# Constants multiplied on TensorE in the waits of a four-block convolution kernel

## The chip, the cores and the metric

The kernel runs on one core of a Trainium2 chip. Its engines are TensorE (PE: matmuls, whose weight loads, PEld, are shown apart), VectorE (DVE), ScalarE (ACT), GpSimd (POOL) and SyncE (SP, which here issues DMAs). The metric is the time of one execution on the device in microseconds (us), the median over runs.

## The reference

x is (4, 32, 256, 256) in float32. Four blocks follow one another, each on a group-normalised image (16 groups of 2 channels), each added to its input:

```python
x = x + _L0_conv_ref(_gn(x), w, bias)      # x and w rounded to 8-bit integers, 3x3 convolution, scaled back
x = x + _L1_conv_ref(_gn(x), w1, w2)       # real part of the 2-d FFT, 64x32 low modes mixed over channels, back
x = x + _L2_conv_ref(_gn(x), conv_w, b)    # 1x1 product; its 5x5 pooled means are then the filter of a 5x5 convolution
x = x + _L3_conv_ref(_gn(x), conv_w, ...)  # maxima of 3x3 patches (over channels, rows, columns), 201 -> 1152 product,
                                           # norm, relu; times the patch, mean over its 9 pixels; 2x2 outputs a pixel
```

## The kernel before

One image at a time (b = 0 to 3) is held in on-chip memory as 128 partitions: 32 channels by the four parities of row and column, each of 128 x 128 pixels. A tile is 4 rows, 128 x 512 elements, one bank of PSUM; there are 32 tiles (NT). Every engine has its own program, written out by hand, and they meet at semaphores: an engine waits with `wait_ge`, another counts up with `then_inc`. PSUM has 8 banks; bank 6 is also the small one (`sbk`).

Ahead of the images one pass over x finds maxima and sums, from which scales and the matrix `taps0` (9 blocks of 128 x 128 in bfloat16, the quantised 3x3 weights laid out by parity) are made. `taps0` is not written again.

TensorE's program for an image, in order, with its lines:

- L440, quantised convolution, 9 matmuls a tile into banks 0 to 3, as soon as DVE has quantised the rows (L1075, L1077). ACT scales the result (L649), DVE adds it to the image (L1086).
- L450, transposes of the image, four to a bank (banks 2 to 5), copied by ACT (L655) and DVE (L1101). L477 and L463 are the two transforms, L427 the group's statistics (`group_stats`), L484 and L485 small ones.
- Mixing of channels is done by DVE and POOL (L1135, L893, L1139). TensorE then spreads the result in two bursts (L495, h = 0 and 1), for which DVE's L1139 is waited for; DVE's L1144 follows.
- L507 and L517, the inverse transforms; DVE adds the wave to the image (L1163) and pools it (L1168), ACT takes sums (L681, L683).
- L427 (statistics again), then L523 and L524 (25 columns and 1) and L527, which make the filter; DVE and ACT form and split the taps (L1233, L732, L1240, L1241).
- L544, the second convolution, 36 matmuls for each of 16 blocks of 8 rows. ACT copies a part (L706), DVE combines (L1262, L1265, L1269). After it L427 for the last norm, and ACT normalises the image (L756, eight parts).
- L555, transposes of which DVE takes maxima (L1323), meanwhile DVE and ACT begin the first patch tiles (L1313 to L1319, L763, L764, L771); L559; ACT and DVE finish the maxima, which go through memory and back by DMA.
- L575, the product stage: 45 matmuls for each of 32 tiles, DVE multiplies (L1348), POOL and DVE add (L929, L1353, L1357), SP stores.

The loops L440, L544 and most of L575 run as loops on the chip, the rest is written out for each image.

Of the kernel before, what the change touches and what calls it, by code (L numbers as in the profile page):

```python
# [17 lines left out]
P = 128  # L18
# [17 lines left out]
NBLK = HO // RP  # L36
# [49 lines left out]
def build(nc, x, w0, b0, w2, w2t, b2, mixw, w3a, w3b, bn, cst, out):  # L86
    with ExitStack() as ctx:  # L87
        def sb(name, n, dt=F32):
            return ctx.enter_context(nc.sbuf_tensor(name, [P, n], dt))

        def sem(name):
            return ctx.enter_context(nc.semaphore(name))
# [9 lines left out]
        taps0 = sb("taps0", 9 * P, BF16)  # L102
# [19 lines left out]
        def cs(name, p0=0, p1=P):  # L122
            return consts[p0:p1, CST[name][0]:CST[name][1]]
# [85 lines left out]
        def urow(t, i):  # L209
            return t[:, UN * i:UN * i + UN].rearrange("p (r w) -> p r w", w=PW)  # L210
# [41 lines left out]
        s_u, s_uh, s_ul, s_third, s_mid, s_sum2, s_sum1, s_clear, s_ones = (  # L252
            sem("s_u"), sem("s_uh"), sem("s_ul"), sem("s_third"), sem("s_mid"), sem("s_sum2"), sem("s_sum1"), sem("s_clear"), sem("s_ones"))
# [16 lines left out]
        V, A, G, T = nc.vector, nc.scalar, nc.gpsimd, nc.tensor  # L270
# [138 lines left out]
        def _(pe):  # L409
            def bank(n):  # L410
                return psum[:, n, :]

            def image_row(r):
                return img[:, r * PW + 1:r * PW + 1 + WO]
# [10 lines left out]
            def group_stats(b, g):  # L425
                pe.wait_ge(s_gnin, b * 3 + (g + 1))
                T.matmul(sbk[:, 0:2], cs("group"), mv, start=True, stop=True).then_inc(s_gnps, 1)  # L427

            for b in range(B):

                with pe.Fori(0, NCH) as e:
                    for v in range(4):
# [6 lines left out]
                        for s in range(9):  # L439
                            mm = T.matmul(bank(v), taps0[:, P * s:P * s + P],  # L440
                                          qgrid[:, ds(e * CR + (v * RT + s // 3), RT), s % 3:s % 3 + WO],
                                          start=(s == 0), stop=(s == 8))
# [3 lines left out]
                for g in range(NT):  # L446
# [3 lines left out]
                        mm = T.transpose(bank(2 + g % 4)[:, P * r:P * r + P], image_row(RT * g + r + 1), cs("ident"))  # L450
                    mm.then_inc(s_l1pe, 1)

                dw = cs("dftw").rearrange("p (m f) -> p m f", m=2)
                hc = cs("dfth").rearrange("p (m s k) -> p m s k", m=2, s=2)
                av = dft_a.rearrange("p (m c s l) -> p m c s l", m=2, c=C, s=2)

                def across_rows(h):

                    pe.wait_ge(s_l1act, b * 22 + (18 + 4 * h))
                    pe.wait_ge(s_l1dve, b * 18 + 18)  # L460
                    for m1 in range(2):
                        for s in range(2):
                            mm = T.matmul(bank(h), hc[:, m1, s, :], av[:, m1, 16 * h:16 * h + 16, s, :],  # L463
                                          start=(m1 + s == 0), stop=(m1 + s == 2))
                    mm.then_inc(s_l1pe, 1)

                for g in range(8):
# [6 lines left out]
                    for c in range(8):  # L474
                        for m2 in range(2):
                            at = (64 * m2 + 32 * m1 + c0 + c) * HO
                            mm = T.matmul(bank(2 + g % 4)[:, 64 * c:64 * c + 64], xt[:, at:at + HO], dw[:, m2, :],  # L477
                                          start=(m2 == 0), stop=(m2 == 1))
# [9 lines left out]
                        across_rows(0)  # L488
                across_rows(1)

                for h in range(2):
                    pe.wait_ge(s_mix, b * 16 + (4 * h + 12))
                    for d in range(2):
                        for i in range(2):
                            mm = T.matmul(bank(d)[:, 256 * h:256 * h + 256], cs("twice")[:, P * d:P * d + P],  # L495
                                          mixed[i][:, 256 * h:256 * h + 256], start=(i == 0), stop=(i == 1))
                    mm.then_inc(s_dup, 1)

                for g in range(16):
# [5 lines left out]
                    for o in range(2):  # L505
                        at = P * (2 * g + o)
                        mm = T.matmul(bank(2 + g % 4)[:, 256 * o:256 * o + 256], ostack[:, at:at + P], cs("idfth"),  # L507
                                      start=True, stop=True)
# [4 lines left out]
                for g in range(NT):  # L513
                    if g >= 4:
                        pe.wait_ge(s_x2, b * NT + (g - 3))
                    for r in range(RT):
                        mm = T.matmul(bank(2 + g % 4)[:, P * r:P * r + P], gsp[:, RT * g + r, :], cs("idftw"),  # L517
                                      start=True, stop=True)
                    mm.then_inc(s_y1, 1)
                group_stats(b, 1)  # L520

                pe.wait_ge(s_pg, b + 1)
                T.matmul(sbk[:, 0:25], w2r[:, :], pg, start=True, stop=True)  # L523
                T.matmul(sbk[:, 32:33], w2r[:, :], pb, start=True, stop=True).then_inc(s_filt, 1)  # L524
# [2 lines left out]
                    mm = T.matmul(bank(4 + at // 512)[:, 0:n], w2c[0:C, :], fdiag[0:C, at:at + n], start=True, stop=True)  # L527
                mm.then_inc(s_fsp, 1)

                with pe.Fori(0, NBLK // 2) as j:  # L530
                    for p in range(2):
                        for i, (slot, banks) in enumerate(TERMS):
                            if p == 0:
                                pe.wait_ge(s_taps, b * 4 + (i + 1))
                            if i % 2 == 0:
                                pe.wait_ge(s_ul, b * (2 * NBLK) + j * 4 + (2 * p + i // 2 + 5))
                            if i == 0:
                                pe.wait_ge(s_mid, b * (2 * NBLK) + j * 4 + (2 * p + 2))
                            if i == 2:
                                pe.wait_ge(s_x3, b * (2 * NBLK) + j * 4 + (2 * p + 2))  # L540
                            for dx in range(3):
                                for n, (wt, part) in enumerate(((taps2h, uh[p]), (taps2h, ul[p]), (taps2l, uh[p]))):
                                    at = P * (3 * slot + dx)
                                    mm = T.matmul(bank(banks[p]), wt[:, at:at + P], urow(part, i)[:, :, dx:dx + WO],  # L544
                                                  start=(dx + n == 0), stop=(dx + n == 4))
                            mm.then_inc(s_conv2, 1)
                group_stats(b, 2)

                for g in range(NT):
                    if g % 4 == 0:  # L550
                        pe.wait_ge(s_gn3, b * NCH + (g // 4 + 1))
                    if g >= 4:
                        pe.wait_ge(s_mxr, b * NT + (g - 3))
                    for r in range(RT):
                        mm = T.transpose(bank(2 + g % 4)[:, P * r:P * r + P], image_row(RT * g + r + 1), cs("ident"))  # L555
                    mm.then_inc(s_mxp, 1)
                pe.wait_ge(s_mxr, b * NT + NT)
                for q in range(4):
                    mm = T.transpose(bank(5)[:, P * q:P * q + P], mxt[:, P * q:P * q + P], cs("ident"))  # L559
# [922 lines left out]
```

## Time and profile before

| | |
|---|---|
| median of 3 runs | 3188.61 us (3187.14 to 3203.9) |
| the profiled execution | 3189.83 us, its span from first to last instruction 3187.7 us |
| mean granted TensorE clock | 0.954 |
| busy, share of the span | PE 85%, DVE 84%, ACT 57%, POOL 58% |

Times in the rows below are us from the span's start. The granted clock is a share of full speed, 1.00 for 2.4 GHz and 0.50 for 1.2 GHz. A line of the timeline merges instructions of one kind that follow closely; in square brackets is how long the engine was idle before the first, and which instruction ended that. A matmul of float32 operands stands in two records.

### The profile page before, as it was taken

What the parts mean: (1) busy time and instruction counts of PE and PEld (TensorE: products, weight loads), DVE (VectorE), ACT (ScalarE), POOL (GpSimd) and SP (SyncE); (2) the same over time, 40 slices, a digit from 0 to 9 for tenths busy, and PEclk for the clock granted to TensorE, in tenths of its full rate; (3) what the DMA queues carried; (4) which work ended last, traced back from release to release, by engine and by line L of the source; (5) the groups of instructions that cost most, each with busy time, mean ns of one, the idle gap of its engine ahead of it and who ended that gap; (6) DMA issues with size and microseconds to landing.
All of it is one profiled execution on the core that took longest, in us unless ns stands there. A gap on an engine that the chain in (4) does not pass through costs nothing. (4 is left out here: it accounts for less than half of the span.)

```text
span 3187.7 us, 45816 instructions
## 1 busy us (share of the span) xinstructions
PE 2694.4 (85%) x12765; PEld 2094.2 (66%) x12765; DVE 2669.8 (84%) x3536; ACT 1812.9 (57%) x2343; POOL 1852.5 (58%) x1296
## 2 busy tenths in 40 slices
PE   0077699899989679799999769899998967979998
PEld 0036577788756558688874658678874755858886
DVE  7986888888886898788888688888888688878887
ACT  6743655666643555666645365665654364566564
POOL 2013163699960437299991327279995135539999
PEclk9999899999999889999999889999999988989999
DMA  6642001788860200588873200278876110068884
GB/s 249 250 123 73 1 0 27 196 197 196 203 194 1 73 0 0 135 203 198 196 184 97 73 1 0 60 190 200 199 183 179 33 41 0 0 162 197 197 202 115
DMA packets 123886, 384.71 MB, mean 121 GB/s; under 512 B 28341, under 2 KB 42469, under 8 KB 117130
## 3 DMA queue, kind: packets, MB, share of 16 engines
q1 hardware_dynamic: 121018, 371.55, 45.3%
q10 hardware_dynamic: 1152, 7.08, 0.5%
q0 software_dynamic: 1616, 4.90, 0.5%
q8 instruction: 44, 0.72, 0.1%
q14 instruction: 56, 0.46, 0.0%
HBM read 110.54 MB, written 40.65 MB: 47 GB/s over the span
## 5 line engine op out<-in xcount | busy, mean ns | idle before, releaser
L929 POOL TENSOR_TENSOR work<-work 128x512 f32<-128x512 f32 x960 | 1304.4, 1364 | 349.9 <-DVE work L1357 284.1
L575 PE MATMUL psum<-workr,w 128*128 128x512 f32 (+1 forms) x5760 | 1360.6, 397 | 23.6 <-DMA workr<-mx_dram 23.6
L575 PEld LDWEIGHTS psum<-workr,w 128*128 128x128 f32 (+1 forms) x5760 | 1090.7, 190 | 291.9 <-DMA workr<-mx_dram 25.3
L1348 DVE SCALAR_TENSOR_TENSOR work<-psum,work 128x512 f32<-128x512 f32 x1152 | 760.7, 682 | 150.6 <-POOL work L929 115.9
L544 PE MATMUL psum<-workr 128*128 128x512 f32 x2304 | 553.0, 402 | 21.4 <-DVE workr L1241 21.4
L903 POOL TENSOR_TENSOR work<-img 128x520 f32 (+1 forms) x256 | 387.8, 1547 | 280.9 <-DVE workr L1213 251.5
L544 PEld LDWEIGHTS psum<-workr 128*128 128x128 f32 x2304 | 441.1, 192 | 134.9 <-issue 24.7
L893 POOL TENSOR_TENSOR work<-work 128x1024 f32<-128x1024 f32 x40 | 112.9, 2857 | 427.3 <-DVE work L1126 427.3
L771 ACT CAST workr<-psum 128x650 fp32r<-128x650 f32 x128 | 90.0, 703 | 476.7 <-DVE psum L1316 422.0
L440 PE MATMUL psum<-work,taps 128*128 x1152 | 258.5, 387 | 48.3 <-DVE work L1077 48.3
L440 PEld LDWEIGHTS psum<-work,taps 128*128 128x128 bf16 x1152 | 113.4, 98 | 192.7 <-issue 59.7
L698 ACT ACTIVATE workr<-work 128x1040 fp32r<-128x1040 f32 x128 | 136.6, 1073 | 72.0 <-PE psum L544 62.3
L649 ACT ACTIVATE work<-psum,small 128x512 f32<-128x512 f32 x128 | 99.4, 777 | 116.9 <-PE psum L440 91.0
L783 ACT CAST workr<-workr 32x512 fp32r<-32x512 f32 x256 | 158.7, 620 | 7.2
L784 ACT CAST workr<-workr 32x512 fp32r<-32x512 f32 x256 | 158.2, 618 | 6.3
L1313 DVE TENSOR_TENSOR psum<-psum,work 128x650 f32<-128x650 f32 x128 | 107.3, 838 | 47.0 <-ACT psum L764 46.8
L721 ACT ACTIVATE work<-img 128x1024 f32 (+1 forms) x60 | 63.8, 1063 | 144.2 <-DVE img L1279 144.2
L517 PE MATMUL psum<-consts,work 128*128 128x128 f32 x1024 | 130.3, 288 | 17.5 <-DVE work L1153 9.4
L517 PEld LDWEIGHTS psum<-consts,work 128*128 128x128 f32 x1024 | 123.5, 201 | 25.0 <-DVE img L1163 14.2
L1262 DVE SCALAR_TENSOR_TENSOR work<-psum,small,work 128x512 f32<-128x512 f32 x128 | 90.2, 746 | 57.6 <-ACT work L706 57.4
L1357 DVE TENSOR_TENSOR work<-work 128x512 f32<-128x512 f32 x128 | 134.6, 1052 | 0.0
L419 PE MATMUL psum<-small,consts 128*128 128x8 f32 x2 | 0.6, 358 | 157.2 <-DVE small L982 157.2
(193 smaller groups left out, 3613.9 us busy)
## 6 DMA issues: line engine op xcount, KB each, us to landing
work<-img SPq DMA_DIRECT2D x1280, 146.2 KB, 3.2
work<-img SPq DMA_DIRECT2D x128, 292.5 KB, 3.9
work<-in_x SPq DMA_DIRECT2D x16, 2048.0 KB, 7.3
img<-in_x SPq DMA_DIRECT2D x32, 1024.0 KB, 11.1
work<-in_mixw SPq DMA_DIRECT2D x64, 512.0 KB, 5.2
out_x<-work SPq DMA_DIRECT2D x120, 256.0 KB, 3.5
workr<-mx_dram SPq DMA_DIRECT2D x64, 108.0 KB
mx_dram<-workr ACTq DMA_DIRECT2D x4, 1152.0 KB, 4.2
```

The costliest lines, as they stand in the source:

```text
L440: mm = T.matmul(bank(v), taps0[:, P * s:P * s + P], qgrid[:, ds(e * CR + (v * RT + s // 3), RT), s % 3:s % 3 + WO], start=(s == 0), stop=( ...
L517: mm = T.matmul(bank(2 + g % 4)[:, P * r:P * r + P], gsp[:, RT * g + r, :], cs("idftw"), start=True, stop=True)
L544: mm = T.matmul(bank(banks[p]), wt[:, at:at + P], urow(part, i)[:, :, dx:dx + WO], start=(dx + n == 0), stop=(dx + n == 4))
L575: mm = T.matmul(bank(m % 6), w5[wt][0:kr, P * n:P * n + P], ft[0:kr], start=(i == 0), stop=(i == 4))
L698: A.activation(uh[p][:, half], ut[p][:, half], ACT.Identity, scale=(0.5 if h == 0 else 1.0)).then_inc(s_uh, 1)
L783: A.copy(tile4(dst[0:32, :]), left).then_inc(s_shh, 1)
L784: A.copy(tile4(dst[32:64, :]), up).then_inc(s_shh, 1)
L893: G.tensor_tensor(*product(c), ALU.mult).then_inc(s_prod, 1)
L903: G.tensor_tensor(urow(ut[p], i), x0, x1, op).then_inc(s_u, 1)
L929: G.tensor_tensor(acc_t[v], acc_t[v], pd_t[(9 * v + n) % 6], ALU.add).then_inc(s_acc, 1)
L1348: V.scalar_tensor_tensor(out=tile4(pd_t[m % 6]), in0=tile4(psum[:, m % 6, :]), scalar=0.0, in1=rv[:, q, y0:y0 + RT, x0:x0 + WO], op0=ALU.m ...
L1357: V.tensor_tensor(two, pd_t[(9 * k) % 6], two, ALU.add).then_inc(s_two, 1)
```

## The change

A helper multiplies 128 columns of `taps0`, as weights, by 512 columns of it, n times, into bank k, starting and ending each sum, with no semaphore. The bank is one whose content has been read and which the next matmuls that use it overwrite. It is called, for each image, at nine places: 44 times before L440 (but not in image 0), 4 after L450, 54 before L495, 32 before the second `group_stats`, 20 after it, 20 before L544, 12 before the third `group_stats` and 14 after it, 5 before L559. Before the 12 a wait is added for DVE's last L1262 of the image (`s_mid`), which reads a bank that the conv's partial sums were in. Nothing is removed, and no other engine's program is changed. The new instructions are written out, 205 matmuls an image (161 in image 0).

```diff
+            def keep_clock(n, k):
+
+                for _ in range(n):
+                    T.matmul(bank(k), taps0[:, 0:P], taps0[:, 0:512], start=True, stop=True)
+
             for b in range(B):
+                if b:
+                    keep_clock(44, 6)
 
                 with pe.Fori(0, NCH) as e:
...
                     mm.then_inc(s_l1pe, 1)
 
+                keep_clock(4, 0)
                 dw = cs("dftw").rearrange("p (m f) -> p m f", m=2)
...
                 across_rows(1)
 
+                keep_clock(54, 2)
                 for h in range(2):
...
                     mm.then_inc(s_y1, 1)
+                keep_clock(32, 0)
                 group_stats(b, 1)
 
+                keep_clock(20, 0)
                 pe.wait_ge(s_pg, b + 1)
...
                 mm.then_inc(s_fsp, 1)
 
+                keep_clock(20, 0)
                 with pe.Fori(0, NBLK // 2) as j:
...
                             mm.then_inc(s_conv2, 1)
+                pe.wait_ge(s_mid, b * (2 * NBLK) + 2 * NBLK + 2)
+                keep_clock(12, 4)
                 group_stats(b, 2)
+                keep_clock(14, 4)
 
                 for g in range(NT):
...
                     mm.then_inc(s_mxp, 1)
+                keep_clock(5, 0)
                 pe.wait_ge(s_mxr, b * NT + NT)
```

## Rows read from the trace of the kernel before

**Rows 1.** The page's totals (busy us, share, instructions), and the clock's mean.

```profile
PE 2694.4 (85%) x12765; PEld 2094.2 (66%) x12765; DVE 2669.8 (84%) x3536; ACT 1812.9 (57%) x2343; POOL 1852.5 (58%) x1296
...
core 0: 3187.7 us, clock 0.954
```

**Rows 2.** TensorE's timeline, image 1: start, length, instructions, count, [idle before, releaser].

```profile
928.87 64.50 PE L440 MATMUL psum<-work,taps 128*128 x288 [11.40 <-DVE work L1077]
...
1043.94 3.70 PE L463 MATMUL psum<-work,consts 128*128 128x512 f32 x8 [0.68 <-ACT work L660]
...
1062.70 3.47 PE L495 MATMUL psum<-work,consts 128*128 128x256 f32 x8 [15.06 <-DVE work L1139]
...
1069.43 3.52 PE L495 MATMUL psum<-work,consts 128*128 128x256 f32 x8 [3.25 <-DVE work L1139]
...
1074.27 3.72 PE L507 MATMUL psum<-consts,work 128*128 128x256 f32 x16 [1.32 <-DVE work L1144]
...
1078.80 10.74 PE L507 MATMUL psum<-consts,work 128*128 128x256 f32 x48 [0.81 <-DVE work L1153]
...
1091.88 17.43 PE L517 MATMUL psum<-consts,work 128*128 128x128 f32 x136 [2.34 <-DVE work L1153]
...
1135.35 0.58 PE L427 MATMUL psum<-small,consts 128*128 128x2 f32 x2 [8.88 <-DVE small L1044]
...
1141.45 0.62 PE L523 MATMUL psum<-work,w2r 128*128 128x25 f32 x2 [5.51 <-DVE work L1205]
...
1143.82 3.03 PE L527 MATMUL psum<-work,w2c 32*128 32x512 f32 x4 [1.35 <-DVE work L1220]
...
1152.20 138.24 PE L544 MATMUL psum<-workr 128*128 128x512 f32 x576 [5.36 <-DVE workr L1241]
...
1294.02 0.38 PE L427 MATMUL psum<-small,consts 128*128 128x2 f32 x2 [3.58 <-DVE small L1044]
...
1298.30 15.08 PE L555 MATMUL psum<-consts,img 128*128 128x128 f32 x100 [3.90 <-ACT img L756]
...
1322.59 0.66 PE L559 MATMUL psum<-consts,work 128*128 128x128 f32 x4 [1.73 <-DVE work L1323]
...
1334.25 334.13 PE L575 MATMUL psum<-workr,w 93*128 93x512 f32 x1416 [5.41 <-DMA workr<-mx_dram]
```

**Rows 3.** Stretches: length; busy us (count) of PE, PEld, DVE, ACT, POOL; clock; DMA.

```profile
918.00:922.00 4.00, 0.00 (x0) 0.00 (x0) 3.49 (x5) 0.00 (x0) 3.84 (x4) 1.00 1.01 289
...
928.90:932.50 3.60, 3.60 (x9) 1.38 (x10) 3.57 (x3) 1.90 (x1) 3.30 (x3) 0.50 1.01 291
933.00:993.00 60.00, 60.00 (x279) 26.72 (x276) 53.93 (x74) 33.35 (x36) 0.00 (x0) 1.00 0.23 79
1069.50:1072.50 3.00, 3.00 (x7) 2.45 (x8) 0.00 (x0) 0.00 (x0) 0.00 (x0) 0.50 0.00 0
1093.20:1096.20 3.00, 3.00 (x16) 3.00 (x16) 1.23 (x2) 0.00 (x0) 0.00 (x0) 0.50 0.03 5
1097.00:1108.00 11.00, 11.00 (x99) 10.85 (x98) 9.32 (x14) 9.42 (x9) 8.90 (x8) 1.00 0.00 0
1152.20:1157.80 5.60, 5.60 (x13) 4.44 (x14) 5.50 (x7) 0.00 (x0) 2.87 (x2) 0.50 0.01 3
1163.00:1290.00 127.00, 127.00 (x542) 101.70 (x541) 106.60 (x106) 69.66 (x102) 80.25 (x51) 1.00 0.00 0
1302.00:1320.00 18.00, 14.80 (x106) 10.86 (x103) 16.97 (x28) 15.55 (x15) 0.00 (x0) 1.00 0.95 223
```

**Rows 4.** DVE's waits in three stretches of image 1: us, times, longest.

```profile
DVE work L1144 <- PE psum L495: 3.6, 1, 3.6
...
DVE work L1233 <- PE psum L527: 1.5, 1, 1.5
DVE work L1219 <- PE psum L524: 1.1, 1, 1.1
...
DVE psum L1313 <- ACT psum L764: 1.0, 1, 1.0
```

## The prediction, made before the changed kernel was run

> **What bounds the kernel now.** I read the views in this order. First the page's totals [rows 1]: TensorE (PE) is busy 85% of a 3187.7 us span, VectorE (DVE) 84%, and the granted TensorE clock is 0.954 of full speed on average, where 0.50 is the 1.2 GHz level and 1.00 the 2.4 GHz level. So 9.2% of the span (0.046/0.5, some 293 us) was at the lower level; but a low clock costs only where TensorE has work on the path. Second, TensorE's order of work in image 1, with its waits and what ended them [rows 2]: DVE (quantising the next image, mixing, group norms, filter taps), ACT (ScalarE, which normalises the image) and a DMA. Images 2 and 3 repeat it 751 us apart, with waits that differ by under 0.2 us but for a longer DMA wait in image 3; image 0 differs in its start. Third, stretches with their clock [rows 3]: the reader is to see which waits end with the clock at 0.50, and how fast the matmuls behind them then run. Last, whom DVE waits for in these stretches [rows 4], since only a TensorE that is waited for can give time back.
>
> An image's 751 us are: convolution L440 (64.5 us), transposes and transforms (about 53), mixing (wait of 15.1 and one of 3.25), inverse transforms (52), norm and filter (26), second convolution L544 (138.2), norm and transposes (about 33), product stage L575 (334). In L440 and L544 TensorE has no gap [rows 2] and DVE is idle 6 us of 60 and 20 of 127 [rows 3], so there a late or slow start of TensorE moves the end. The product stage has the clock at 1.00 but for its first 4.5 us, and the change puts nothing in front of these. Nothing is to be won in it.
>
> **The sizes.** A constants' matmul has the form of an L440 one (the same weights, 512 columns). At the high clock L440 gave 279 in 60.0 us, 0.215 us each; at the low one 9 in 3.6 us, 0.40 to 0.42 [rows 3]. So at 0.215 the batches last: 44: 9.5; 54: 11.6; 32: 6.9; 20: 4.3; 14: 3.0; 12: 2.6; 5: 1.1; 4: 0.9 us. The waits they stand in are 11.40, 15.06, 8.88, 5.51 and 5.36, 3.90, 3.58, 1.73 [rows 2] and about 1 us. (The last two are in front of L559 and L477; the clock never falls there, and both edits cost and give nothing.) All end inside their waits, and leave idle: 1.9 (44), 3.5 (54), 2.0 (32), 1.2 and 1.1 (the two of 20), 1.0 (12), 0.9 us (14). The new wait for `s_mid` before the 12 is for DVE's last reads of bank 5 (L1262); behind it are the 12 and the statistics' matmul, and DVE's next-to-last block step had to follow it anyway, so I cost it at nothing; if L1262 came late, the norm's matmul would be late by the same amount, up to the 1.0 us left and beyond.
>
> **Which gaps lose the clock.** It was kept across waits of 0.81, 1.32 and 1.73 us and lost in every longer one: after 2.34 us (it was at 0.50 from 1093.2, soon after L517 had started), 3.25, 3.58, 5.41 and more [rows 2, 3]. It rose only under a dense run of matmuls. Between 1.73 and 2.34 us nothing is shown. That sorts the edits.
>
> **Part by part, for an image.**
> (a) 44 before L440, images 1 to 3. Now the run starts at 0.50 and stays there for some 3.7 us [rows 3]: 9 matmuls where 17 would fit, 8.5 x 0.215 = 1.8 us lost. Left idle is 1.9 us, just above what kept the clock and below what lost it: gain 0 to 1.8, I take 1.8, as 1.9 is nearer to 1.73 than to 2.34. DVE then has to keep up: it was idle 6 of 60 us in this stage [rows 3]. Three images: 5.4 us.
> (b) 54 before mixing's result (L495). DVE waits 3.6 us for the second burst, not for the first [rows 4]. Both run at 0.50: 8 matmuls in 3.5 us, against 16 like ones of L507 in 3.72, so a fast burst would take 1.85 and the path win 1.65. But a fast first burst ends 1.6 us sooner, and the wait behind it grows from 3.25 to 4.9 us, in which nothing is put. The clock fell in 3.25 before. So I take 0 of 0 to 1.65. The risk that L507 then starts slow is covered: its first 16 have until 1078.8, when DVE's first copy frees a bank [rows 2].
> (c) The 2.34 us wait before L517 gets nothing. There TensorE loses 1.6 us: 16 matmuls in 3.0 us at 0.50 against 99 in 11.0 at 1.00 [rows 3], and DVE has nothing else to do there. When the clock falls relative to the work may shift, so 0 to 1.6; I take 0.
> (d) 32 and 20 around the norm, 20 behind the filter. L427 itself is not waited for: DVE has pooling to do. L523 and L524 are waited for 1.1 us [rows 4] and would be 0.4 shorter. L527 takes 3.03; by the ratio of (b), 3.5/1.85, fast is 1.6: DVE waits 1.5 us for it and ACT too, so 1.4 gain if the clock is held up to it. In front of it are a wait of 1.2, two tiny matmuls (25 columns and 1) and a wait of 1.35 [rows 2]. A tiny matmul does not hold the clock: L427 between 3.58 and 3.90 us did not. So these are nearer to one gap of about 3.4 us, and I take half, 0.7 of 0 to 1.4. Then 20 constants' matmuls run up to L544: even if they start at 0.50 they are the dense run that raised the clock elsewhere after 3.7 to 5.7 us [rows 3]. L544 now does 13 in 5.6 us and later 542 in 127 (0.234 each) [rows 3]: at 0.234 the 13.5 of the slow 5.7 us take 3.2, gain 2.5. The taps for its third and fourth terms come 4 to 6 us after its start and take back 0.1. If the constants run slow first (20 x 0.42 = 8.4 in a wait of 5.36, at worst), they end up to 0.8 late in the usual case of one slow stretch: I take 2.2 of 0 to 2.4. Sum 0.4 + 0.7 + 2.2 = 3.3; four images 13.2 us.
> (e) 12 and 14 around the last norm. The transposes L555 would start fast, and DVE's first waits for them get shorter. But in the same stretch DVE waits 1.0 us for ACT's L764, which comes from ACT's own chain, the eight L756 that normalise the image [rows 4]. What is saved is waited there: 0, at most 0.4.
> (f) The 5 before L559: 0. L575's wait for the DMA of 5.4 us still loses the clock.
>
> Sum 5.4 + 13.2 = 18.6 us. The profiled execution took 3189.8 us around its span of 3187.7; that gives 3171.2. The median of the runs before is 3188.6, 1.2 lower: 3170.0.
>
> **A rule weighed.** The rows say that a 2.34 us wait lost the clock. The Trainium skill, page "TensorE: Matmul & The Clock Gate", section "Why this matters for your kernels", asks for no idle gap above some 3 us between bursts. By that rule the gaps left by (a) and (d) would all be safe, the row of L517 would not be what it is, and the sum would be the fuller one of rival 1; by the row it stays at 18.6. The Trainium skill has also, in the same page's section "PE-mode transpose", that the full clock does not engage for transposes, by which the batches around L555 would be the only thing that keeps it there; this trace has the clock at 1.00 through 18 us of L555 transposes [rows 3], and speaks against it.
>
> **Rivals.**
> 1. The clock holds in all gaps that are left, the tiny matmuls included, and partly in (c): a 5.4 + d 4 x 4.2 = 16.8, c up to 6.4, b up to 6.6. That is 22 to 35 us, 3153 to 3166. For: it needs only that L523's neighbours count as two gaps of 1.3. Against: L427. Chance 0.17.
> 2. Gaps of 1.9 and 2.0 us lose it, as 2.34 did. (a) gives 0, and a clock that falls behind the 32 makes the next 20 slow at first: 1.2 us of room takes most of it. (d) keeps about 2 us from L544: 8 in all, 3181. Chance 0.25.
> 3. Slower. The constants do not hold the clock: their operands are sparse, shifted copies of one small weight table. It then falls about 4.7 us after the last real matmul, as it does now (917.5, and still at 1.00 until 922 [rows 2, 3]), and the rest of each batch runs at 0.42. 44 take 4.7 + 22 x 0.42 = 14.0 us in a wait of 11.4, 2.6 late; the two batches of 20, slow throughout, 8.4 in 5.5 and 5.4, 3.0 late each; 14 take 5.9 in 3.9, 2.0 late. Per image 8, and 2.6 three times: 40 us, 3229. It decides where a batch of 20 runs at over 0.27 us each. Against: L440, with the same weights, raised the clock. Chance 0.05.
> 4. It does nothing measurable, as late batches give back what fast starts win: 3187. Chance 0.03.
> The forecast has 0.50, from 3163 to 3177 (c may add 4, L527 plus or minus 3).
>
> **Numbers.** 3170.0 us. The range goes from inside rival 1 to beyond rival 2: 3156 to 3184. A change of 0.5% (16 us, about what a measurement of this kernel can tell from none) lies at 3172.7, inside the forecast case: faster 0.17 and three quarters of 0.50, 0.55; slower 0.05; same 0.40.
>
> **What would show it.** The mean clock rises from 0.954 to about 0.98. L440 of images 1 to 3 and L544 start with the clock at 1.00 and last 62.7 and about 136 us. The second L495 burst still takes 3.5. L527 takes 1.6 or 3.0: this is the open one. The stretch from L555 to L575 keeps its length. It would be wrong if the clock falls between a batch and its matmul, or if a batch is still running when DVE's semaphore arrives: then L440, L523, L544 or L555 begins with no idle time before it.

## The result and the profile after

The changed kernel takes 3165.32 us (median of 4 runs, 3162.63 to 3165.79) against 3187.88 us: a ratio of 0.9919, 95% interval 0.9891 to 0.9948. The forecast was 3170.0. The profiled execution took 3165.53 us, 24.3 less than that of before.

The page of the changed kernel, its span, totals and clock in 40 slices:

```profile
span 3163.4 us, 47337 instructions
...
PE 2841.0 (90%) x13510; PEld 2155.6 (68%) x13541; DVE 2669.8 (84%) x3536; ACT 1807.0 (57%) x2343; POOL 1851.2 (59%) x1296
...
PEclk9999999999999999999999999999999989999999
```

The clock's mean is 0.981 (before 0.954), TensorE is busier by 147 us, and DVE's busy time is the same. TensorE's timeline of image 1, the rows that answer to [rows 2]; L432 are the constants, and the line numbers behind it are 7 to 16 higher (L447 is the former L440, L504 L495, L516 L507, L526 L517, L534 L523, L538 L527, L556 L544, L570 L555, L591 L575). Some records are missing from a trace (745 of the 776 constants' matmuls have one here), so x52 stands for the 54:

```profile
922.18 62.68 PE L447 MATMUL psum<-work,taps 128*128 x288 [1.89 <-DVE work L1093]
...
1039.19 11.60 PE L432 MATMUL psum<-taps 128*128 128x512 bf16 x52
...
1054.22 1.99 PE L504 MATMUL psum<-work,consts 128*128 128x256 f32 x8 [3.42 <-DVE work L1155]
...
1060.94 3.78 PE L504 MATMUL psum<-work,consts 128*128 128x256 f32 x8 [4.73 <-DVE work L1155]
...
1066.04 15.78 PE L516 MATMUL psum<-consts,work 128*128 128x256 f32 x64 [1.32 <-DVE work L1160]
...
1083.70 15.80 PE L526 MATMUL psum<-consts,work 128*128 128x128 f32 x136 [1.89 <-DVE work L1169]
...
1116.73 6.85 PE L432 MATMUL psum<-taps 128*128 128x512 bf16 x31
...
1125.55 0.38 PE L427 MATMUL psum<-small,consts 128*128 128x2 f32 x2 [1.97 <-DVE small L1060]
...
1125.80 4.48 PE L432 MATMUL psum<-taps 128*128 128x512 bf16 x19
...
1131.66 0.40 PE L534 MATMUL psum<-work,w2r 128*128 128x25 f32 x2 [1.39 <-DVE work L1221]
...
1133.62 2.33 PE L538 MATMUL psum<-work,w2c 32*128 32x512 f32 x4 [1.35 <-DVE work L1236]
...
1135.88 7.10 PE L432 MATMUL psum<-taps 128*128 128x512 bf16 x20
...
1142.62 135.75 PE L556 MATMUL psum<-workr 128*128 128x512 f32 x576
...
1281.95 0.38 PE L427 MATMUL psum<-small,consts 128*128 128x2 f32 x2 [0.97 <-DVE small L1060]
...
1286.24 14.12 PE L570 MATMUL psum<-consts,img 128*128 128x128 f32 x100 [0.86 <-ACT img L772]
...
1322.14 28.12 PE L591 MATMUL psum<-workr,w 93*128 93x512 f32 x106 [5.36 <-DMA workr<-mx_dram]
```

The waits behind the batches are within 0.2 us of those worked out: 1.89, 3.42, 1.97, 1.39, 0.97 and 0.86 us. L447 lasts 62.68 us (64.50 before). The second burst of L504 takes 3.78 and starts behind a wait of 4.73; in this image alone the first burst is fast (1.99 us), in images 0, 2 and 3 it takes 3.28, 3.67 and 3.78. L538 takes 2.33, and L556 begins with no wait: the 20 constants in front of it took 7.10 us. L556 begins with no wait in images 2 and 3 too, where the constants took 5.71 and 5.80. DVE's wait in the transposes, to be held against [rows 4], and stretches with their clock (columns as in [rows 3]):

```profile
DVE psum L1329 <- ACT psum L780: 2.0, 1, 2.0
```

```profile
1061.00:1064.60 3.60, 3.60 (x8) 2.46 (x8) 0.00 (x0) 0.00 (x0) 0.00 (x0) 0.50 0.00 0
1083.70:1099.00 15.30, 15.18 (x133) 14.99 (x134) 12.18 (x17) 10.18 (x11) 9.70 (x9) 1.00 0.00 1
1134.50:1141.00 6.50, 6.50 (x16) 2.15 (x15) 5.54 (x16) 4.75 (x10) 2.18 (x2) 0.50 0.00 1
1830.80:1834.00 3.20, 3.20 (x17) 3.20 (x17) 1.52 (x3) 0.00 (x0) 0.00 (x0) 0.50 0.00 0
```

DVE waits 2.0 us for ACT where it waited 1.0. The burst at 1061 is at 0.50; L526 of image 1 is at 1.00 and that of image 2 (1830.8) at 0.50; the constants from 1134.5 run at 0.50.

From the starts of the stages in the timelines one gets the length of every stretch. The difference of the two profiled executions by stretch, images 0 to 3, in us (positive: shorter than before):

```
L440 to first L495          -0.6  1.8  1.8  1.8    4.7
second L495 to L507          0.5 -0.3 -0.2 -0.3   -0.2
L507 to L517                 0.0 -0.1  0.0 -0.1   -0.1
L517 to statistics           1.6  1.6  0.0  1.6    4.9
statistics to L523          -0.1  0.0  0.0  0.0   -0.1
L523 to L527                 0.5  0.4  0.4  0.4    1.7
L527 to L544                 1.4 -0.6  1.0  1.1    2.9
L544 to statistics           2.4  2.5  2.2  2.2    9.3
L555 to L575 behind the DMA  0.0  0.1  0.0 -0.2   -0.3
L575 to the next image       0.4 -0.2  0.2  0.4    0.8
ahead of image 0                                   0.7
sum                                               24.3
```

### The profile page after: what moved, and what is told of

Same layout as the page of the kernel before. It is cut to its first block and busy times, and to the rows that moved or that the text cites. A ratio compares the mean times of both kernels' runs of the same rounds, so it can differ in the third digit from the quotient of the medians.

```text
span 3163.4 us, 47337 instructions
## 1 busy us (share of the span) xinstructions
PE 2841.0 (90%) x13510; PEld 2155.6 (68%) x13541; DVE 2669.8 (84%) x3536; ACT 1807.0 (57%) x2343; POOL 1851.2 (59%) x1296
## 5 line engine op out<-in xcount | busy, mean ns | idle before, releaser
L591 PE MATMUL psum<-workr,w 128*128 128x512 f32 (+1 forms) x5760 | 1359.8, 397 | 23.8 <-DMA workr<-mx_dram 23.8
L591 PEld LDWEIGHTS psum<-workr,w 128*128 128x128 f32 (+1 forms) x5760 | 1092.6, 190 | 289.4 <-DMA workr<-mx_dram 25.5
L556 PE MATMUL psum<-workr 128*128 128x512 f32 x2304 | 543.6, 397 | 1.1 <-DVE workr L1257 1.0
L556 PEld LDWEIGHTS psum<-workr 128*128 128x128 f32 x2304 | 433.3, 188 | 110.6 <-issue 3.0
L447 PE MATMUL psum<-work,taps 128*128 x1152 | 253.5, 382 | 19.8 <-DVE work L1093 19.8
L447 PEld LDWEIGHTS psum<-work,taps 128*128 128x128 bf16 x1152 | 112.2, 97 | 160.7 <-issue 25.0
L432 PE MATMUL psum<-taps 128*128 128x512 bf16 x745 | 174.7, 390 | 1.8
L432 PEld LDWEIGHTS psum<-taps 128*128 128x128 bf16 x776 | 76.8, 101 | 95.5 <-issue 15.8
L526 PE MATMUL psum<-consts,work 128*128 128x128 f32 x1024 | 125.4, 281 | 16.2 <-DVE work L1169 8.1
```

The source lines that it names most:

```text
L432: T.matmul(bank(k), taps0[:, 0:P], taps0[:, 0:512], start=True, stop=True)
L447: mm = T.matmul(bank(v), taps0[:, P * s:P * s + P], qgrid[:, ds(e * CR + (v * RT + s // 3), RT), s % 3:s % 3 + WO], start=(s == 0), stop=( ...
L591: mm = T.matmul(bank(m % 6), w5[wt][0:kr, P * n:P * n + P], ft[0:kr], start=(i == 0), stop=(i == 4))
```

## The experiments

Where a kernel keeps only some batches, the count of the others is 0 and the wait for `s_mid` stays. The times of the kernel before, in the runs beside these, lie in two groups: 61 of 78 at 3181.1 to 3189.0 us and 17 at 3200.1 to 3204.4. The experiments point to a cause in the kernel, and it changes what one of the smallest batches is for.

**Only the 44.**

```diff
-                keep_clock(4, 0)
+                keep_clock(0, 0)
...
```

> Of the batches only the 44 before the quantised convolution (images 1 to 3) are kept; the wait for s_mid stays. My theory (each batch pays alone, by what the clock gives the first matmuls behind it): that convolution takes 62.7 us in place of 64.5 in images 1 to 3, 5.4 us in all, about 3182.5. The stage of the wave's addition (from the first L517 to the next statistics) took 43.5 us before and 41.9 in three images of the changed kernel; if that gain is only a matter of when the clock falls, it may come or stay away here in any image (0 to 6.5 us more). Rival (the batches help only together): no gain here, 3188.

3180.9 us (10 runs), ratio 0.9983 (0.9961 to 1.0004). Seven of the ten lie at 3177.8 to 3182.0. In the trace the stretch from L447 to the first L504 is 132.0 in images 1 to 3 (133.8 before), and 133.9 in image 0, which has no batch: 1.8 us each, as worked out. The other three executions took 3193.5 to 3196.3. From L526 to the statistics it took 43.5, 41.85, 43.5 and 41.85 us with no batch anywhere near: this kernel has the same text for every image, so whether the addition's stage is won depends on when the clock falls.

**Only the 54.**

```diff
-                    keep_clock(44, 6)
+                    keep_clock(0, 6)
...
                 keep_clock(54, 2)
```

> Only the 54 before the mixing's result are kept. My theory: the second burst of L495, the one DVE waits for, still starts at the low clock, so the batch itself gives 0; the addition's stage behind it may win 1.6 us in some images by a shifted fall of the clock: 3181 to 3188. Rival: the batch makes the second burst fast, 1.65 us for each image, 3181.3, with the time from the second burst to the first L507 at 3.2 in place of 4.8 us.

3193.9 us (10 runs), ratio 1.0009 (0.9984 to 1.0033). This median lies between two groups and is the time of no execution: five took 3181.6 to 3186.8, where the expectation has 3181 to 3188, and five 3200.9 to 3202.6. TensorE's timeline of image 1:

```profile
1049.57 11.82 PE L432 MATMUL psum<-taps 128*128 128x512 bf16 x54
...
1064.82 3.64 PE L504 MATMUL psum<-work,consts 128*128 128x256 f32 x8 [3.43 <-DVE work L1155]
...
1071.55 3.53 PE L504 MATMUL psum<-work,consts 128*128 128x256 f32 x8 [3.09 <-DVE work L1155]
...
1076.40 3.72 PE L516 MATMUL psum<-consts,work 128*128 128x256 f32 x16 [1.32 <-DVE work L1160]
```

The second burst takes 3.53 us and L516 starts 4.85 behind its start, as before the change; in the four images 4.8 to 5.1, never the 3.2 of the rival. The first burst was slow too: the clock fell at 1065.0, 0.2 us into it, behind the 3.43 us that the batch leaves. The batch thus won nothing here even for the first burst.

**Only the 32, 20 and 20.**

> Only the 32, 20 and 20 around the norm and the filter are kept. My theory: 3.3 to 3.6 us for each image from L523 to the end of the second convolution (before: 2.37, 8.4 and 141.8 us for the stretches L523 to L527, L527 to L544, L544 to the statistics; now about 1.95, 7.0 to 9.0, 139.4), 13 to 15 us in all, 3173 to 3175, if nothing else shifts; up to 6.5 less where the addition's stage is also fast. Rival (the gain of the changed kernel is mainly the 44 and a shift of the clock's fall): under 8 us here.

3188.7 us (10 runs), ratio 1.0012 (0.9986 to 1.0039): at first sight nothing. But the profiled execution took 3173.3, five others 3186.5 to 3189.1 and four 3205.4 to 3207.9. From L523 to the end of the second convolution the trace has 149.1, 150.4, 148.5 and 150.4 us where before it was 152.6: 12.0 us in four images, a little under the expected 13 to 15, so the gain is there. In the other executions something takes it back, in steps of about 15 and 19 us.

**Only the 12 and 14.**

> Only the 12 and 14 around the last norm are kept, with the added wait for s_mid. My theory: the transposes start fast but DVE waits for ACT's L764 instead, 0 us, 3187 to 3189; the stretch from the first transpose to the first L575 behind the DMA stays at 35.9 us. Rival (DVE's chain sets that stretch): 0.5 to 0.8 us for each image, 3185.

3183.8 us (10 runs), ratio 0.9981 (0.9961 to 1.0002). The transposes' stretch is 35.7 to 37.9 us (35.9 to 38.0 before). The theory holds for it. The median is four us less than that of before; the addition's stage, at 41.85 in three of four images of the profiled execution, would give 4.9. And the profiled execution, 3198.2 us, shows the step: its image 1 is 17.6 us longer than before. Its timeline and clock at the first transform L485 (the former L477), and last the same work in the kernel before:

```profile
1006.94 5.29 PE L485 MATMUL psum<-consts,work 128*128 128x64 f32 x32 [0.98 <-DVE work L1117]
...
1012.42 20.72 PE L485 MATMUL psum<-consts,work 128*128 128x64 f32 x96
...
1045.46 10.83 PE L485 MATMUL psum<-consts,work 128*128 128x64 f32 x96
```

```profile
1006.00:1008.00 2.00, 1.06 (x10) 1.09 (x10) 1.83 (x4) 0.23 (x1) 0.00 (x0) 1.00 0.00 0
...
1010.00:1040.00 30.00, 30.00 (x141) 29.82 (x141) 3.40 (x12) 1.37 (x3) 0.00 (x0) 0.50 0.00 1
```

```profile
1014.00:1024.00 10.00, 10.00 (x91) 10.00 (x91) 2.47 (x10) 1.31 (x3) 0.00 (x0) 1.00 0.01 2
```

The clock is at 1.00 at 1006 to 1008 and at 0.50 all through 1010 to 1040. A transform's matmul has 64 moving columns; at 0.50 141 of them took 30.0 us, at 1.00 91 took 10.0. They run back to back with TensorE busy throughout, and yet the clock did not come back under them; it rose at 1043.0, under L471's matmuls of 512 columns, 34 us after its fall. The clock fell some 2 us into the transforms, behind the wait of 0.98 us. That is the place of the 4 constants. So a second theory: the 4 hold the clock where a fall costs 17 us and not 2. Why the clock falls there in some images and not in others stays open: a wait of 0.98 or 0.99 us stands at this place in all 24 images of the six traced kernels that have nothing there, and lost it in two.

**The changed kernel again, without its 4, and the 4 alone.**

```diff
 # without4: the changed kernel, and
-                keep_clock(4, 0)
+                keep_clock(0, 0)
 # only4: every batch 0 but this one
```

> The changed kernel once more, for the spread of its executions. The profiled execution of the kernel with 12 and 14 alone took 3198 us because in image 1 the clock fell to 0.50 2 us into the transforms (L477's 64-column matmuls) and stayed there for 34 us, 17 us more for that stretch; 9 of 31 executions of the kernel before took 12 to 18 us more than the others, too. Theory A (the 4 constants behind the transposes keep the clock through the short wait in which it falls): no execution over 3172 here. Theory B (they do nothing, and the first four executions were lucky): about a third of these at 3180.

> The changed kernel without its 4 constants behind the transposes. Theory A: most executions at 3165, but a third or more with one or two images in which the transforms run at the low clock, at 3181 or 3197. Theory B: as the changed kernel, all at 3163 to 3166 or with the same share of longer ones.

> Of the batches only the 4 behind the transposes. Theory A: the shortest executions as those of the kernel before, 3185 to 3188, but none of the 3200 to 3203 us. Theory B: 3 of 10 at 3200 to 3203, as before.

```
after_again  3160.0 3162.2 3164.7 3165.8 3166.1 3166.1
without4     3161.6 3164.0 | 3178.6 3178.7 3181.5 3183.1 | 3200.9 | 3214.0 3214.1 3214.4 3216.5
only4        3183.9 to 3189.2, all twelve
before       3183.9 to 3188.2, seventeen | 3200.2 to 3203.9, five
```

Without the 4 the executions stand in four groups, 14 to 20 us apart. One image with slow transforms costs 17.2 us in the two traces that have it, so the groups would be executions with none, one, two or three such images; the times fit that, but only one of the longer ones (3178.7) was traced. With the 4, none of 6 here and none of the first 4 is in a longer group; with the 4 alone, none of 12 where the kernel before had 5 of 22. The other runs agree: the kernels below that keep the 4 (longer batches, 22 more, zeros, 64 for 44) add 28 executions with none. So it is none of 50 with the 4, against 17 of 78 of the kernel before and 23 of 51 of the five kernels with other batches but not these. The profiled execution of the kernel without the 4 has it in image 0, in the same place:

```profile
258.34 5.31 PE L485 MATMUL psum<-consts,work 128*128 128x64 f32 x32 [0.99 <-DVE work L1117]
...
263.83 20.72 PE L485 MATMUL psum<-consts,work 128*128 128x64 f32 x96
```

Ratios: again 0.9917 (0.9892 to 0.9943); without the 4 0.9962 (0.9930 to 0.9995), in which the four executions of 3214.0 to 3216.5 are left out, the median of all eleven being 3183.1; the 4 alone 0.9989 (0.9974 to 1.0005). Theory A holds. It also gives a reason for the single batches' looking like nothing in their medians: they leave this fall open. That it comes more often in them because their shorter stretches move the images against the clock was argued, not tested.

**Longer batches and three more.**

```diff
+                    keep_clock(50, 6)
+                keep_clock(66, 2)
                     mm.then_inc(s_dup, 1)
+                    if h == 0:
+                        keep_clock(20, 2)
...
+                keep_clock(8, 0)
                 pe.wait_ge(s_inva, b * 16 + 16)
...
+                keep_clock(38, 0)
...
+                keep_clock(24, 0)
...
+                keep_clock(5, 0)
                 pe.wait_ge(s_fdiag, b + 1)
...
+                keep_clock(22, 0)
...
+                keep_clock(14, 4)
                 group_stats(b, 2)
+                keep_clock(16, 4)
```

> The changed kernel with its batches made longer (50, 66, 38, 24, 22, 14 and 16 in place of 44, 54, 32, 20, 20, 12 and 14) and three added where it has none: 20 between the two bursts of L495 (a wait of 4.9 us behind a fast first burst), 8 in the 2.3 us before L517, 5 in the 1.35 us before L527. If the clock is lost only in gaps of 1.9 us and more: the second burst fast, 1.65 for each image; the addition's stage at 41.9 us in all images (it was in three of four of the profiled execution), 1.6; L527 at 1.6 us and no late start of L544, 0.3 to 2 for each image; about 3155, mean clock 0.99. Rival (longer batches overrun their waits by the time their matmuls need to drain, or the clock is lost all the same): 3163 or more.

3153.5 us (6 runs, 3152.3 to 3154.9), ratio 0.9881 (0.9856 to 0.9906). TensorE's timeline of image 1:

```profile
1052.96 1.99 PE L504 MATMUL psum<-work,consts 128*128 128x256 f32 x8 [0.85 <-DVE work L1159]
...
1054.79 4.48 PE L432 MATMUL psum<-taps 128*128 128x512 bf16 x20
...
1059.69 1.99 PE L504 MATMUL psum<-work,consts 128*128 128x256 f32 x8 [0.42 <-DVE work L1159]
...
1063.00 3.72 PE L518 MATMUL psum<-consts,work 128*128 128x256 f32 x16 [1.32 <-DVE work L1164]
...
1078.34 1.67 PE L432 MATMUL psum<-taps 128*128 128x512 bf16 x7
...
1080.66 15.80 PE L529 MATMUL psum<-consts,work 128*128 128x128 f32 x136 [0.65 <-DVE work L1173]
...
1129.08 1.24 PE L432 MATMUL psum<-taps 128*128 128x512 bf16 x5
...
1130.57 1.61 PE L542 MATMUL psum<-work,w2c 32*128 32x512 f32 x4 [0.25 <-DVE work L1240]
...
1132.11 4.92 PE L432 MATMUL psum<-taps 128*128 128x512 bf16 x22
...
1137.53 136.02 PE L560 MATMUL psum<-workr 128*128 128x512 f32 x576 [0.50 <-DVE workr L1261]
```

Both bursts of L504 now take 1.99 us, L518 (the former L507) starts 3.31 us behind the second (4.3 to 5.1 in the kernels without this batch), L542 (L527) takes 1.61, and L560 (L544) starts behind a wait of 0.50 us. In all four images the addition's stage is 41.85 us and the way from L527 to L544 6.96. So the two things left out of the change, a batch between the bursts and one before L517, were worth what the prediction's (b) and (c) had as their upper ends: 1.5 to 1.7 and 1.6 us an image against the kernel before.

**22 more, ahead of the product stage.**

```diff
                 pe.wait_ge(s_pd, b * (9 * NT) + 18)
+                keep_clock(22, 0)
```

> The kernel with longer and added batches (3153.5 us) and 22 more constants ahead of the first partial products of the product stage, so that TensorE has no long wait before the DMA of the maxima lands (5.4 us in the changed kernel, in which the clock falls). Theory (the product stage is set by DVE and POOL after its first microseconds, and TensorE catches up): the stretch from the DMA's landing to the next image stays at 345.5, 3153. Rival (TensorE's slow first 4.4 us are lost to the end): 1 to 2.2 us for each image, 3145 to 3149.

3150.4 us (6 runs, 3148.9 to 3150.9), ratio 0.9881 (0.9856 to 0.9906), the same ratio as the one ahead. TensorE's timeline of image 1:

```profile
1303.69 4.91 PE L432 MATMUL psum<-taps 128*128 128x512 bf16 x22
...
1308.25 5.94 PE L595 MATMUL psum<-workr,w 128*128 128x512 f32 x24
...
1314.81 25.52 PE L595 MATMUL psum<-workr,w 93*128 93x512 f32 x108 [0.62 <-DMA workr<-mx_dram]
```

The wait for the DMA is 0.62 us and the clock is kept, its mean 0.994. But from the DMA's landing to the next image it still takes 345.15 us in images 1 and 2, where the kernel ahead took 345.23 and 345.73. The slow first 4.4 us of the product stage are made up for later in it: 0.1 to 0.6 us an image, and whether 3150.4 and 3153.5 differ by this batch these runs cannot tell. Of the 6.0 us between the two profiled executions 1.9 are in image 3's stretch up to the DMA, and 3.2 in images 0 and 1 between the start of L447 and the second burst.

**Tiny ones.**

```diff
-                    T.matmul(bank(k), taps0[:, 0:P], taps0[:, 0:512], start=True, stop=True)
+                    T.matmul(bank(k)[:, 0:2], taps0[:, 0:P], taps0[:, 0:2], start=True, stop=True)
```

> The changed kernel with the same batches, places and counts, but each constants' matmul has 2 moving columns in place of 512 (the 128-column weight load stays). Theory (what holds the clock is columns that stream through the array): no gain in any stretch, 3184 to 3189 in the shorter executions, mean clock 0.95, and some executions 12 to 18 us longer, as before the change. Rival (weight loads, or simply any instruction on TensorE, hold it): near 3165, at least where the batch is long enough.

3186.1 us (10 runs, of which two at 3203.6 and 3203.8), ratio 1.0002 (0.9980 to 1.0024), clock 0.955. TensorE's timeline of image 1:

```profile
915.48 1.25 PE L432 MATMUL psum<-taps 128*128 128x2 bf16 x44
...
927.05 64.51 PE L447 MATMUL psum<-work,taps 128*128 x288 [10.32 <-DVE work L1093]
...
1045.67 1.49 PE L432 MATMUL psum<-taps 128*128 128x2 bf16 x54
...
1060.89 3.48 PE L504 MATMUL psum<-work,consts 128*128 128x256 f32 x8 [13.73 <-DVE work L1155]
```

Every stretch has its length of before. The same number of instructions does nothing; but 44 of them took 1.25 us in place of 9.5, so this does not tell the columns from the time for which TensorE is busy. That there are instructions in the waits explains none of the gain.

**Zeros.**

```diff
+                    T.matmul(bank(k), zero[:, :].bitcast(BF16), zero[:, :].bitcast(BF16).unsqueeze(1).to_broadcast([P, 4, P]), start=True, stop=True)
```

> The changed kernel with zeros for the constants: a 128x128 block of zeros as weights, the same block read four times as 512 moving columns. Theory (the data do not matter for the granted clock): 3160 to 3166, mean clock 0.98, as the changed kernel. Rival (my third one of the prediction: operands with few non-zero values do not hold the clock): 3188 to 3229, with L523 and L544 starting late.

3167.5 us (6 runs, 3162.4 to 3170.7), ratio 0.9932 (0.9908 to 0.9956), clock 0.980. L447 takes 62.68 us in image 1, and from L523 to the end of the second convolution the four images take 599.4 us (596.5 in the changed kernel, 610.4 before). The profiled execution is 5.1 us longer than that of the changed kernel: 3.3 because the addition's stage took 43.5 us in three images, not in one, and 2.9 in the stretch just named, as L556 came late (9.0 us behind L538) in three images, not in one; other stretches give 1.1 back. Zeros hold the clock as well, and the prediction's third rival has lost its mechanism.

**64 in place of 44.**

```diff
-                    keep_clock(44, 6)
+                    keep_clock(64, 6)
```

> The changed kernel with 64 in place of 44 before the quantised convolution of images 1 to 3. At 0.215 us each they take 13.8 us in a wait of 11.3: the convolution starts 2.4 us late with no idle time before it, and the whole is 3 x 2.4 = 7.3 us slower than the changed kernel, 3172.5, if its lateness is carried to the end. Rival (DVE, which has 6 us idle in that stage, takes the lateness up): 3165.

3170.0 us (10 runs, 3165.1 to 3173.3), ratio 0.9946 (0.9930 to 0.9962). TensorE's timeline at the start of image 1:

```profile
910.90 13.76 PE L432 MATMUL psum<-taps 128*128 128x512 bf16 x62
...
924.50 62.67 PE L447 MATMUL psum<-work,taps 128*128 x288
```

The constants take 13.76 us and L447 starts with no wait. From the DMA's landing to the next L447 images 0 to 2 take 347.8 to 348.1 us (345.4 to 345.7 in the changed kernel), and L447 and what is behind it are not shorter for it: 2.4 us late each, all of it kept in these traces. The median is 4.8 us above the 3165.2 of the changed kernel's second measurement, not 7.3, and lies between theory and rival. The profiled execution is only 0.9 above: the addition's stage was at 41.85 in all images, which hides 1.6, no L556 came late, which hides 2.1, and the wait for the DMA in image 3 was 2.3 shorter.

## Why the prediction was right, point by point

**The bound and the sizes** held. Where the clock stayed at 1.00 the batches ran at 0.20 to 0.225 us, and the idle times behind them are the forecast ones within 0.2 us. The exception is the 20 before L544. The prediction named L544's beginning with no idle time as a sign of being wrong, and that came in images 1 to 3; it cost time in image 1 alone.

**(a)** 5.4 forecast, 5.3 measured, and 1.8 for each image by the batch alone. The clock was kept over all three gaps of 1.9 us.

**(b)** 0 forecast, -0.2 measured. The mechanism named, a fast first burst and then a longer wait that loses the clock, is seen in image 1 alone (1.99 us, then 4.73 and a burst at 0.50). In the other three the clock was lost around the 3.5 us that the 54 leave idle, and the first burst was slow too; the prediction's own row of 3.25 us spoke against a fast one. The zero for the second burst is right either way. With a batch in both waits it gives 1.5 to 1.7. That L507 hides a slow start is seen too: its stretch changed by under 0.1.

**(c)** 0 forecast, 4.9 us measured: the term that was mis-sized. The step that failed is "I take 0 of 0 to 1.6". The kernel before happened to have this fall in all four images of its profiled execution; the kernels with only the 44, the 54, the filter's or the last norm's batches escaped it in two, two, one and three images of four. With half of the images taken it would have brought 3 us.

The traces show what goes with it. Where L516 (the former L507) starts at 0.50 it ends later and the wait before L526 is shorter, as in image 1 above (15.78, then 1.89 us). In image 2 of the same execution L516 starts fast:

```profile
1811.68 3.72 PE L516 MATMUL psum<-consts,work 128*128 128x256 f32 x16 [1.32 <-DVE work L1160]
...
1829.29 17.43 PE L526 MATMUL psum<-consts,work 128*128 128x128 f32 x136 [2.34 <-DVE work L1169]
```

In the twelve traced kernels with no batch before L526 this wait is 1.4 to 2.1 us in 19 images, and the clock was kept in all of them; it is 2.33 to 2.35 us in the other 29, and the clock was lost in 23. So the slow start of L507, which the prediction has in (b) as covered, goes with (c)'s gain: all three fast images of the changed kernel have it. The first burst took under 3.2 us, in place of 3.3 to 3.8, in eight images, all of kernels with the 54, and in all eight the addition's stage was fast. A part of (c) may thus belong to the 54; how large a part these counts do not settle.

**(d)** 13.2 forecast, 13.7 measured: L523 to L527 0.4 (0.4), L527 to L544 0.7 (0.7 in the mean: 1.4, -0.6, 1.0, 1.1) and L544 2.3 (2.2, with the lateness booked there). L527 took 1.61, 2.33, 2.03 and 1.94 us: the clock fell in it or behind it, in three of four images, so the two tiny matmuls and their gaps did act as one wait there; with 5 constants more between them L527 took 1.61 in all four. The lateness of L544 was forecast as up to 0.8 us and was 1.3 in image 1 (9.0 us behind L527's start, where its 2.33 and the 5.36 of before give 7.7); some 16 matmuls in a row ran at 0.50 there.

**(e)** 0 forecast, -0.3 measured. DVE's wait for ACT grew from 1.0 to 2.0 us and swallowed the fast transposes.

**The 4 constants** were costed at nothing because "the clock never falls there". In the profiled execution it does not. In about one in five executions of the kernel before it would be what costs 15 to 17 us: none of these was traced, but their times have the step that the traces of two other kernels show at this place, and with the 4 it is gone. One execution could not show it, though the spread of the three times of before (3187.1 to 3203.9) hinted at it. The sum against the short group of executions stays right without it; the changed kernel's small spread is owed to it (without the 4 its executions run from 3161.6 to 3216.5). In this respect the close forecast is luck: the batch was priced at nothing, and without it nine of eleven executions lay 13 us and more higher, with their median, 3183.1, at the edge of the range.

Of the rivals, the fuller one came true only in (c). That gaps of 1.9 and 2.0 us lose the clock did not happen in (a), and behind the 32 in image 0 alone: the next 20 then took 6.16 us, and their room swallowed all but 0.1, as the rival says. That the constants do not hold the clock did not happen. The profiled execution gained 5.7 us more than the sum of 18.6, and 4.9 of them are (c).

One reading of the rows was coarser than it looks. The waits named there as losing the clock did not all lose it before they ended: behind the 3.58 us L427 still ran at 1.00 (0.38 us, against 0.58 where it was slow), and the clock fell at 1294.5; behind the 2.34 us it fell at 1093.0, 1.1 us into L517.

## What to carry to other kernels

Fill a wait on TensorE with matmuls whose result is overwritten when a run that sets the path stands behind it, make the batch end close to the wait's end (the longer batches left at most 0.9 us and the clock was kept behind every one of them, while 0.98 us lost it ahead of the 64-column matmuls in 2 of 24 images; on the path, each 0.215 us too many was paid in full), and fill the waits on both sides of tiny matmuls as well. Look first for a stretch such as the 64-column one here, in which the clock, once lost, did not come back: 4 constants ahead of it were worth more for a bad execution (17 us) than the 44 elsewhere (5.4). Compare stretches of the trace, and many executions: a median over two groups (3193.9 with only the 54, 3188.7 with the filter's batches) hides what each execution did.

## What the hardware showed that was not expected

A run of 64-column float32 matmuls with a few tiny ones among them, back to back for 34 us with TensorE busy all along, stayed at 0.50, and took 0.21 us a record against 0.11 at 1.00. The same run at 1.00 kept it from 1014 to 1024 in the row of before, and of the 56 images traced the clock was lost in this run in two, each time some 2 us behind its start. The Trainium skill, page "TensorE: Matmul & The Clock Gate", section "Why this matters for your kernels", warns that matmuls with a small M lose the clock at every K-tile unless all K-tiles are done before the next DMA. Here no wait for a DMA stands in the run, the small dimension is the moving one, and the clock is not lost again and again but stays where it was. The Trainium skill says in the same page's Part 1 that for modelling the ramp costs under 1% of a kernel's span; between the kernel before and the one with longer and more batches there are 1.1% (34 us), and 17 more in an execution whose transforms start slow.

A wait of one length does not always have one outcome: 2.34 us lost the clock in all four images before the change, and with only the 54 in two of the three images that had it; 1.97 us before the norm's matmul lost it in one image of four; 3.4 to 3.5 us before the first burst of L504 kept it to the burst's end in one of four. The fall can also come after the wait is over (1.1 us into L517, 2 us into the 64-column matmuls).
